# Four places of a four-layer chain: dispatch, start of the soft experts, their pairs, and the end of the last feed-forward

## The reference, cut to what matters

```
x = x + L0_xattn(layernorm(x), ctx)          # x: 8 batches x 256 tokens x 128
x = x + L0_soft_moe(layernorm(x))            # touched
x = x + L1_xattn(...);  x = x + L1_moe(...)  # 64 experts, top 8
x = x + L2_xattn(...);  x = x + L2_moe(...)
x = x + L3_xattn(...);  x = x + L3_ffn(layernorm(x))   # touched

# L0_soft_moe: E=16 experts, S=64 slots, F=256
x = layernorm(x) * g + b;  se = layernorm(slot_embeds) * scale
logits = x @ se.T                                  # b, n, (e s)
dispatch = softmax over the tokens n;  combine = softmax over (e s)
slots = dispatch.T @ x                             # b, e, s, d
eout = (gelu(slots @ Wg + bg) * (slots @ Wu + bu)) @ Wd + bd
return combine @ eout

# L3_ffn: hidden 512
act_quant(x) = clip(round(x * s), -128, 127) / s,  s = 127 / clip(max|x|, 1e-5)   # per token
weight_quant: weights in {-1, 0, 1} times a scale
h = act_quant(x) @ weight_quant(w1).T
h = silu(depthwise_conv1d(h, 3 taps, padding 1) + bias)
return act_quant(h) @ weight_quant(w2).T
```

## Time and profile before

| | us |
|---|---|
| median of 3 runs | 932.74 (932.28 to 936.21) |
| the profiled execution's own time | 932.12 |
| its span | 930.3 |
| dispatch, first transposes to last slots product | 91.6 to 161.1 |
| soft experts, first to last gate and up product | 163.7 to 254.0 |
| layer 3's feed-forward, first `first3` to last output | 873.5 to 928.3 |

### The profile page before, as it was taken

The page is one execution under the profiler, slowest core; times in us unless marked ns, Lnnn a source line. Parts: engine busy times, 40 slices in busy tenths (PEclk is TensorE's granted clock), DMA queues, the critical chain, the costliest instruction groups (busy, mean ns, idle before and its releaser), DMA issues.

```text
span 930.3 us, 16069 instructions
## 1 busy us (share of the span) xinstructions
PE 874.5 (94%) x4762; PEld 674.0 (72%) x4762; DVE 703.4 (76%) x1613; ACT 525.4 (56%) x1007; POOL 584.7 (63%) x575
## 2 busy tenths in 40 slices
PE   7897999999998889999999999999999999998897
PEld 5565775666687856788888888888888776775775
DVE  6997776999745789876666666666668768898896
ACT  3555666455571255666666666666666674446365
POOL 5922444677722235777777777777778777898710
PEclk9999999999999999999999999999999998999998
DMA  6000000222100000200000000000002000000001
GB/s 200 2 2 1 1 1 1 81 67 68 45 2 29 1 9 2 69 26 20 25 23 25 25 25 25 20 25 23 25 25 102 1 1 1 1 1 0 2 12 35
DMA packets 27431, 24.45 MB, mean 26 GB/s; under 512 B 3483, under 2 KB 24179, under 8 KB 27251
## 3 DMA queue, kind: packets, MB, share of 16 engines
q1 hardware_dynamic: 27379, 23.80, 8.5%
HBM read 22.74 MB, written 1.05 MB: 26 GB/s over the span
## 4 chain that ended last, share of the span: by engine, by line
PE 70%; DVE 17%; POOL 5%; ACT 5%; issue 2%; DMA 1%; DVEq 0%; SPq 0%; ACTq 0%; POOLq 0%
PE psum L1918 65%; POOL hh L744 3%; DVE arena L1826 2%; ACT hh L872 2%; PE psum L2086 2%; DVE stats L1368 1%; DVE arena L1466 1%; DVE arena L1463 1%; ACT arena L933 1%; PE psum L2163 1%; DVE arena L1475 1%; PE psum L1979 1%; DVE xn L1387 1%; POOL rstd L655 1%; PE psum L1948 1%
## 5 line engine op out<-in xcount | busy, mean ns | idle before, releaser
L1918 PE MATMUL psum<-xw 128*128 128x512 f32 x1248 | 324.3, 396 | 3.9 <-DVE xw L1521 2.6
L707 POOL TENSOR_TENSOR hh<-arena,hh 128x512 fp32r<-128x512 f32 x176 | 228.4, 1298 | 81.3 <-ACT hh L872 80.0
L1918 PEld LDWEIGHTS psum<-xw 128*128 128x128 f32 x1248 | 233.5, 189 | 56.3 <-issue 7.2
L1726 DVE TENSOR_TENSOR psum<-psum,arena 128x512 f32<-128x512 f32 x176 | 123.0, 699 | 97.7 <-PE psum L1918 91.4
L1102 ACT ACTIVATE arena<-psum 128x512 f32<-128x512 f32 x176 | 105.6, 600 | 120.1 <-PE psum L1918 120.0
L872 ACT ACTIVATE hh<-arena 128x512 fp32r<-128x512 f32 x228 | 142.2, 625 | 38.5 <-DVE arena L1826 36.0
L1918 PE MATMUL psum<-hh,wdn 128*128 128x512 f32 x528 | 148.4, 390 | 0.2 <-POOL hh L707 0.2
L1731 DVE TENSOR_TENSOR arena<-psum,arena 128x512 f32<-128x512 f32 x176 | 121.7, 691 | 7.6 <-DVE psum L1726 1.7
L1918 PEld LDWEIGHTS psum<-hh,wdn 128*128 128x128 f32 x528 | 98.9, 188 | 21.1 <-POOL hh L707 0.5
L1918 PE MATMUL psum<-arena 128*32 128x128 f32 (+6 forms) x992 | 88.3, 309 | 9.5 <-ACT arena L872 7.9
L872 ACT ACTIVATE arena<-psum 128x512 f32<-128x512 f32 (+6 forms) x85 | 57.5, 689 | 48.7 <-PE psum L1918 19.0
(11 more groups left out here) (297 smaller groups left out, 1491.9 us busy)
## 6 DMA issues: line engine op xcount, KB each, us to landing
egu<-in_w SPq DMA_DIRECT2D x44, 128.0 KB, 2.0
egu<-in_egu SPq DMA_DIRECT2D x16, 256.0 KB, 2.6
edn<-in_w SPq DMA_DIRECT2D x44, 64.0 KB, 1.8
edn<-in_edn SPq DMA_DIRECT2D x16, 128.0 KB, 2.1
arena<-in_w SPq DMA_DIRECT2D x1, 1536.0 KB, 6.7
X<-in_x SPq DMA_DIRECT2D x4, 256.0 KB, 5.5
arena<-in_ctxTd SPq DMA_DIRECT2D x2, 512.0 KB, 6.0
arena<-in_conv SPq DMA_DIRECT2D x1, 768.0 KB, 4.4
```

What stands on the lines that cost most here:

```text
L707: pool.tensor_tensor(hh[:, s % 4, 1, :], h1[:, s % 2, :], hh[:, s % 4, 0, :].bitcast(F32), ALU.subtract).then_inc(hh_lo, 1)
L1726: dve.tensor_tensor(bank(2 + k), bank(2 + k), sil[:, k, :], ALU.mult).then_inc(prod_done, 1)
L1918: return pe.matmul(dst, lhsT=lhsT, rhs=rhs, start=start, stop=stop)
```

## The change

In the dispatch, `ln_stats(1, 3)` moves from the head into iteration 4 of VectorE's loop, `ln_apply`, the transposes and the evacuations of groups 2 and 3 into later iterations, and `brec(0)` ahead of `bmax(2)`. On ScalarE, the first expert's weight cast and the Gelu table's load move into the end of the dispatch loop. The slots' rounded part is made by ScalarE (`slot_high`), for experts 0 and 1 before the last `slots_evac`; VectorE keeps the subtraction (`slot_low`), now behind `shift`. In layer 3 the quantisation scales take fewer operations, the bias subtraction and the first tile's scaling are placed elsewhere on VectorE, the last steps get their own PSUM banks, and the order of the last turns and of turn 2 differs.

```diff
@@ -420,6 +420,7 @@
         xq_done = sem("xq_done")
+        xq_first = sem("xq_first")
         xq_tp = sem("xq_tp")
@@ -510,11 +511,14 @@
+        STEP_BANKS = {LAST3 - 2: 2, LAST3: 4}
+        OUT_BANKS = {LAST3 - 3: 3, LAST3 - 2: 0, LAST3 - 1: 1, LAST3: 5}
         def step_bank(u):
-            return bank(2 if u == LAST3 else 6)
+            return bank(STEP_BANKS.get(u, 6))
         def out_bank(u):
-            return bank(3 if u == LAST3 else 7)
+            return bank(OUT_BANKS.get(u, 7))
@@ -821,7 +825,7 @@
                             .then_inc(bnorm_done, 1)
-                        if k == 3:
+                        if k == 7:
                             ln_power(1, NG - 1)
@@ -951,6 +955,18 @@
+            def gate_up0_high(n, i, k, f):
+                act.wait_ge(egu_in[k], i * 16 + 16)
+                if later(n, 2):
+                    act.wait_ge(eu_ready, n - 1)
+                copy(wgu_pair(f, 0), egu_part(k, f)).then_inc(wgu_hi, 1)
+            def slot_high(e, k):
+                if later(e, 2):
+                    act.wait_ge(eu_ready, e * 2 - 2)
+                copy(xall[:, 0, 512 * k:512 * k + 512], slotsT[:, bass.ds(e, 1), :, :].rearrange("p a b s -> p (a b s)")).then_inc(xh_hi, 1)
@@ -959,26 +975,26 @@
             bexp(0)
-            ln_evac_group(1, 2)
             bexp(1)
...
                     bexp(q + 3)
-                if q == 9:
-                    ln_evac_group(1, NG - 1)
+                if q in (4, 14):
+                    ln_evac_group(1, 2 if q == 4 else NG - 1)
+                if q == 4 * B - 4:
+                    gate_up0_high(0, 0, 0, 0)
+                if q == 4 * B - 2:
+                    load_table(ACT.Gelu)
                 if q >= 4 and q % 4 == 1:
...
-            def gate_up0_high(n, i, k, f):
-                act.wait_ge(egu_in[k], i * 16 + 16)
-                if later(n, 2):
-                    act.wait_ge(eu_ready, n - 1)
-                copy(wgu_pair(f, 0), egu_part(k, f)).then_inc(wgu_hi, 1)
+                if q == 4 * B:
+                    act.wait_ge(slots_sb, 2 * B - 1)
+                    slot_high(0, 0)
+                    slot_high(1, 1)
@@ -1019,13 +1035,14 @@
                         gelu(n, i * 2 + k, f)
+                        if f and not last:
+                            slot_high(i * 2 + (k + 2), k)
                         if f == 0 and later(i, 1):
...
-            gate_up0_high(0, 0, 0, 0)
             expert_pair(0)
@@ -1290,7 +1307,7 @@
                 act.wait_ge(qi_done, 2 * g + 2)
-                for t in range(4 * g, 4 * g + 4):
+                for t in range(4 * g if g else 1, 4 * g + 4):
                     last = act.activation(qa[:, t, :], qa[:, t, :], ACT.Copy, scale=rs3[:, t:t + 1])
@@ -1326,8 +1343,26 @@
             for turn in range(PAIRS + 1):
-                if turn < PAIRS:
+                if turn == 2:
+                    activated(4)
+                    activated(5)
+                    token_high(2)
+                    integers_in(0)
+                    scaled_step(1)
+                    continue
+                if turn == PAIRS - 1:
+                    scaled_step(turn - 1)
                     activated(2 * turn)
+                    integers_in(turn - 2)
+                    activated(2 * turn + 1)
+                    continue
+                if turn == PAIRS:
+                    scaled_step(LAST3 - 1)
+                    scaled_step(LAST3)
+                    for u in range(LAST3 - 2, LAST3 + 1):
+                        integers_in(u)
+                    continue
+                activated(2 * turn)
                 if turn == 1:
@@ -1335,17 +1370,14 @@
                     token_scale(2)
-                if turn < PAIRS and turn != 1:
+                else:
                     activated(2 * turn + 1)
-                if turn in (2, 4):
-                    token_high(turn // 2 + 1)
-                if turn >= 2:
+                if turn == 4:
+                    token_high(3)
+                if turn >= 3:
                     integers_in(turn - 2)
...
                     token_scale(3)
-            scaled_step(LAST3)
-            integers_in(LAST3 - 1)
-            integers_in(LAST3)
@@ -1390,7 +1422,7 @@
-                if t % 4 == 3:
+                if t % 4 == 3 and not (L == 1 and t == NT - 1):
                     ln_stats(L, t // 4)
@@ -1419,10 +1451,8 @@
                 then(dve.tensor_reduce(am3[:, r], xn[:, r, :], AX.X, ALU.max, apply_absolute_value=True))
-                then(dve.tensor_scalar(am3[:, r], am3[:, r], 1e-5, None, ALU.max))
-                dve.tensor_scalar(rs3[:, r], am3[:, r], 1.0 / 127.0, None, ALU.mult)
-                then(dve.reciprocal(qs3[:, r], am3[:, r]))
-                dve.tensor_scalar(qs3[:, r], qs3[:, r], 127.0, None, ALU.mult).then_inc(qi_done, 1)
+                then(dve.tensor_scalar(rs3[:, r], am3[:, r], 1.0 / 127.0, 1e-5 / 127.0, ALU.mult, ALU.max))
+                dve.reciprocal(qs3[:, r], rs3[:, r]).then_inc(qi_done, 1)
@@ -1499,26 +1529,24 @@
             bmax(1)
+            brec(0)
             bmax(2)
-            brec(0)
             for q in range(4 * B):
...
                     bmax(q + 3)
-                if q == 6:
+                if q == 4:
+                    ln_stats(1, NG - 1)
+                if q == 10:
                     ln_apply(1, NG - 1)
-            def slot_halves(e, k):
-                if later(e, 2):
-                    dve.wait_ge(eu_ready, e * 2 - 2)
-                slots_e = slotsT[:, bass.ds(e, 1), :, :].rearrange("p a b s -> p (a b s)")
+            def slot_low(e, k):
                 r = slice(512 * k, 512 * k + 512)
-                dve.tensor_copy(xall[:, 0, r], slots_e).then_inc(xh_hi, 1)
                 dve.wait_ge(xh_hi, e + 1)
-                dve.tensor_tensor(xall[:, 1, r], slots_e, xall[:, 0, r].bitcast(F32), ALU.subtract).then_inc(xh_lo, 1)
+                dve.tensor_tensor(xall[:, 1, r], slotsT[:, bass.ds(e, 1), :, :].rearrange("p a b s -> p (a b s)"), xall[:, 0, r].bitcast(F32),
+                                  ALU.subtract).then_inc(xh_lo, 1)
@@ -1549,18 +1577,18 @@
                         hidden0(n, i * 2 + k, f)
-                        if f and not last:
-                            slot_halves(i * 2 + (k + 2), k)
                         if f and k == 0:
                             shift(i)
+                        if f and not last:
+                            slot_low(i * 2 + (k + 2), k)
                         if f == 0 and k and not last:
...
-            dve.wait_ge(slots_sb, 2 * B)
-            slot_halves(0, 0)
-            slot_halves(1, 1)
+            slot_low(0, 0)
+            slot_low(1, 1)
+            dve.wait_ge(slots_mm, 2 * B)
             least_logits(0)
@@ -1839,11 +1867,13 @@
             attended(1, range(4, 8))
+            dve.wait_ge(w3_hi, 4)
+            dve.tensor_tensor(cbias[C:P], conv_bias[C:P], cbias[C:P].bitcast(F32), ALU.subtract).then_inc(cb_lo, 1)
             token_scales(0)
...
             token_integers(0)
-            dve.wait_ge(w3_hi, 4)
-            dve.tensor_tensor(cbias[C:P], conv_bias[C:P], cbias[C:P].bitcast(F32), ALU.subtract).then_inc(cb_lo, 1)
+            dve.wait_ge(qi_done, 2)
+            dve.tensor_scalar(qa[:, 0, :], qa[:, 0, :], rs3[:, 0:1], None, ALU.mult).then_inc(xq_first, 1)
             denominators(1, 1)
@@ -1859,10 +1889,9 @@
                 then(dve.tensor_reduce(am4[:, r], gt[:, q % 2, ks[0]:ks[-1] + 1], AX.X, ALU.max, apply_absolute_value=True))
-                then(dve.tensor_scalar(am4[:, r], am4[:, r], 1e-5, None, ALU.max))
-                then(dve.reciprocal(qs4[:, r], am4[:, r]))
-                dve.tensor_scalar(rs4[:, r], am4[:, r], wm[:, 1:2], 1.0 / 127.0, ALU.mult, ALU.mult)
-                dve.tensor_scalar(qs4[:, r], qs4[:, r], 127.0, None, ALU.mult).then_inc(qs4_done, 1)
+                then(dve.tensor_scalar(am4[:, r], am4[:, r], 1.0 / 127.0, 1e-5 / 127.0, ALU.mult, ALU.max))
+                dve.reciprocal(qs4[:, r], am4[:, r]).then_inc(qs4_done, 1)
+                dve.tensor_scalar(rs4[:, r], am4[:, r], wm[:, 1:2], None, ALU.mult)
@@ -1903,13 +1932,11 @@
             quant_scale(LAST3 - 1)
-            outputs3(PAIRS - 3)
             quant_scale(LAST3)
             integers(LAST3 - 1)
-            outputs3(PAIRS - 2)
             integers(LAST3)
-            outputs3(LAST3 - 1)
-            outputs3(LAST3)
+            for u in range(LAST3 - 3, LAST3 + 1):
+                outputs3(u)
@@ -2109,12 +2136,10 @@
                         logits_slots(q + 3)
-                if q == 9:
+                if q == 14:
                     ln_transpose(1, NG - 1)
...
-            pe.wait_ge(slots_sb, 2 * B)
@@ -2138,6 +2163,8 @@
                 pe.wait_ge(least_done, b * 4 + 3)
+                if not later(b, 1):
+                    pe.wait_ge(slots_sb, 2 * B)
                 if later(b, 2):
@@ -2592,6 +2619,8 @@
                 pe.wait_ge(xq_done, g + 1)
```

(31 more changed lines are left out.)

## The result

The changed kernel takes 920.13 us (median of 4 runs, 919.0 to 921.19) where the kernel before takes 932.51 in the same comparison (931.66 to 936.21): 0.985 times as long, 95% interval 0.983 to 0.988. The forecast was 919.4 in 915.5 to 926. The profiled execution took 919.0 (span 917.3, forecast 918.8). A second profile of the changed kernel, in another comparison, has a span of 918.4, its runs a median of 919.23 against 932.38.

The account below looks back on a forecast made before the run. TensorE, busy 94% of the span, was taken as the bound, time being won where it waits or runs at half clock. Dispatch 2.1, experts' start 3.3, pairs 5.3 and layer 3 2.6 sum to 13.3 us: 919.4, range 915.5 to 926.

Parts of the forecast that it names:

- the start of the experts: First gate product 2.25 us earlier, least_T(0) 2.9 earlier, another 0.4 before shift_rows(0); together 3.3 us.
- Dispatch: Dispatch term: 1.45 from the earlier start plus 1.2 from the clock less 0.58 for moved statistics, 2.1 us.
- The head: Start of the dispatch: POOL's first normalised block and the first transposes come 1.45 us earlier.
- The clock stays up: Dispatch's start: with shorter idle stretches TensorE's clock no longer falls to half at 93 to 96, worth 1.2 us.
- The pairs: Seven expert-pair intervals fall from 80.96 to 75.6 us, as TensorE's wait for shift goes: a gain of 5.3 us.
- row_evac's wait: Expert pairs: ScalarE's odd-slot cast delays row_evac, so outputs_T costs TensorE 0.35 us (0.2 to 0.65) in six intervals.
- The natural interval: Expert pairs: without the wait for shift an interval is the last one's 10.63 us, 9.76 for the first.
- the going of the wait: Expert pairs: shift placed earlier and two casts off VectorE end TensorE's wait of 1.12 us (1.29 start to start).
- The second rival: VectorE, its subtractions meeting POOL's, bounds the pairs at 10.95 us; pairs give 2 us, total 923.7; chance 0.13.
- Layer 3: Layer 3's feed-forward: front, quantisation scales, turn 2, end and stores together gain 2.6 us, bounds 0.9 and 4.5.
- turn 2: Layer 3: integers_in(0) ahead of scaled_step(1) ends a 1.65 us wait but delays later steps; taken as −0.6 us.
- The slower rival: Pairs: ScalarE's slot cast waits for the up product, delaying row_evac, weight cast and gelu; 937.6 us at 2.6; chance 0.04.

Follow-up runs that it names:

- the undone head: Changed kernel with the dispatch's head as before (last norm group's statistics ahead of the first largest-value pass, brec(0) behind bmax(2)): 920.48 us against 934.3.
- the order with shift behind: Changed kernel with the least-logit reduction (shift) behind the even slot's subtraction again, rounded halves still made by ScalarE: 923.4 us against 934.3.
- the run without POOL's work: Changed kernel with POOL's work cut from the pairs (low weights for 8 of 128 columns, shift's subtraction from the logits behind the last pair): 952.97 us.

## Why the prediction was right, and where it was not

**The whole.** 13.3 us were forecast and the profile has 13.0, but 0.78 of these came ahead of every edit, which is luck: the change made 12.2, and inside it misses in both directions cancel in part. The median, 920.13, lies 1.1 above the profiled execution and not 0.6.

**The bound and the start of the experts** were right: 3.25 against 3.3, with the gate product 0.35 behind the last slots product (forecast 0.3) and least_T(0) 2.84 earlier net of what came before (2.9).

**Dispatch, 1.57 against 2.1.** The head (1.53 for 1.45) and the moved statistics (0.67 for 0.58) were right. "The clock stays up" came true, worth 0.7 and not 1.2; and the reason given for it, a shorter idle stretch, is not borne out by the undone head, where it stays up behind the old idle stretch.

**The pairs, 4.53 against 5.3.** The forecast's 75.6 is what the order with shift behind (75.62) and the run without POOL's work (75.60) measure: wait gone, row_evac's wait added. The natural interval is 10.53 rather than 10.63, row_evac's wait 0.47 rather than 0.35; that these two misses cancel (11.00 against 10.98) is luck. Two steps failed. "The natural interval is the last one", with only row_evac's wait added, leaves VectorE out: with shift ahead its subtraction falls behind POOL's operation (1.76 us instead of 0.88), least_logits behind it meets the next one (2.34), and in every second pair TensorE waits for eo_high. And the going of the wait was put down to the order and the casts together, where the casts alone end it. The second rival had that mechanism: it named 10.95 us of VectorE's load, which is what the pair of 11.29 has, but the pair of 11.00 ahead of it has 9.88; it gave the pairs 2 us where they have 4.53.
**Layer 3, 2.87 against 2.6**, from terms that missed in both directions: turn 2 is +0.25 and not −0.6, the end 2.74 in the two profiles (2.4 to 3.0 over all traces) and not 2.4, the stores −1.13 (−0.4 to −1.4) and not −0.3. SP's last four issues now follow one another over 3.41 us, and the last of them stands 0.89 behind the output.

**The slower rival** did not come: gelu at 202.35 still waits 1.77 us for TensorE, so nothing queued ahead of it on ScalarE holds it back there, and no interval is above 11.30.

## What to carry to other kernels

When a wait is taken away by giving work to another engine and by reordering, test the two alone: here the engine did all of it and the order cost up to 0.8 us. Where a VectorE and a GpSimd operation with on-chip inputs meet, the second one waits: place the one that TensorE needs so that it starts first, by a clear margin. On the receiving engine, place the new work behind whatever TensorE waits for next; that was 0.47 us a pair.

## What the runs showed of the hardware

- The clock can stay at 1.00 or fall to 0.50 after the same 2.30 us of idle TensorE, at the same instruction, in kernels that differ elsewhere. Some places dip in one execution and not in another of the same kernel (near 16 us 1.00 and 0.58 in the two profiles of the changed kernel) or of the same code there (near 291 and 866 us). A dip cost 0.67 us in the dispatch; near 866 it cost 1.17 in the changed order and 0.46 in the old one.
- With filler matmuls in TensorE's last waits it stayed at 1.00, in one trace: 1.25 us for 16 products against 1.66 to 1.92 in ten without.
- VectorE's and GpSimd's operations with on-chip inputs take turns. A subtraction of 128x512 takes 0.68 us alone, 0.88, 1.11 or 1.76 when 0.33, 0.57 or 1.21 us of a GpSimd operation are left as it starts.
- From the last output to the end of the span it took 3.47 us with a last store of 256 KB (one trace), 2.40 to 3.35 with four stores issued one behind another, the last of 64 KB, and 1.96 to 1.98 where that last one was issued at once (three traces).
